# Causal grouped attention: dividing by the row sums on VectorE with 32-block transposes, in place of turning the attended values to tokens and back on TensorE

## What is computed

```python
q = rope(x @ Wq.T + bq); k = rope(x @ Wk.T + bk); v = x @ Wv.T + bv
k = jnp.repeat(k, 4, axis=1); v = jnp.repeat(v, 4, axis=1)
att = jnp.einsum('bhqd,bhkd->bhqk', q, k) / jnp.sqrt(16)
att = jnp.where(causal, att, -jnp.inf)
att = jax.nn.softmax(att, axis=-1)
y = jnp.einsum('bhqt,bhtd->bhqd', att, v)
return y.transpose(0, 2, 1, 3).reshape(b, t, n) @ Wo.T + bo
```

## Time and profile before

| what | value |
|---|---|
| time, median of 3 runs | 1567.59 us (1562.62 to 1567.86) |
| the profiled execution | 1567.11 us, of which span 1565.3 us |
| granted TensorE clock, mean | 0.985 of 2.4 GHz |
| busy over the span: TensorE, VectorE, ScalarE, GpSimd | 92%, 62%, 48%, 36% |
| the stage with the change | about 1075 to 1226 us of the span |
| row maxima start in units 0 to 6 (first L2017) | 1099.58, 1112.49, 1126.84, 1144.32, 1158.66, 1176.15, 1190.47 us |

### The profile page before, as it was taken

How to read it: one execution, slowest core, us unless ns; L and a number is a source line. 1 busy time by engine, 2 the same in 40 slices (tenths; PEclk the granted TensorE clock), 3 DMA queues, 4 the chain that set the end, 5 groups by cost and what they waited for, 6 DMA issues and landing times. The chain is left out here.

```text
span 1565.3 us, 29243 instructions
## 1 busy us (share of the span) xinstructions
PE 1439.8 (92%) x10620; PEld 1117.4 (71%) x10646; DVE 965.8 (62%) x2214; ACT 756.6 (48%) x1877; POOL 561.7 (36%) x556
## 2 busy tenths in 40 slices
PE   6999999999899899899999999998898898988897
PEld 4778777787689767677777766895565596733586
DVE  5666667666575665656565557548655754565663
ACT  5565656656235334343443443452545362598352
POOL 2835629354136254515333101552000173100173
PEclk9999999999999999999999999999999999998998
DMA  4122231222272343303021007335000534121534
GB/s 147 55 90 68 84 101 46 86 63 90 82 313 85 122 130 112 120 6 114 24 74 69 1 1 287 142 120 192 1 1 2 197 102 147 31 60 33 187 99 138
DMA packets 57453, 149.48 MB, mean 95 GB/s; under 512 B 10224, under 2 KB 24688, under 8 KB 57200
## 3 DMA queue, kind: packets, MB, share of 16 engines
q1 hardware_dynamic: 39664, 89.58, 16.7%
q0 software_dynamic: 17664, 58.21, 11.0%
HBM read 104.77 MB, written 38.27 MB: 91 GB/s over the span
## 5 line engine op out<-in xcount | busy, mean ns | idle before, releaser
L145 POOL TENSOR_SCALAR ln_var<-ln_moments 128x4 f32<-128x4 f32 x16 | 4.1, 253 | 403.7 <-DVE ln_moments L130 251.3
L412 POOL DMA_INDIRECT expert_rows<-s_y,s_to_row x92 | 90.9, 989 | 57.9 <-ACT s_y L736 36.9
L1370 ACT ACTIVATE s_scratch<-s_bank,s_neg_max 128x128 f32<-128x128 f32 (+3 forms) x128 | 67.2, 527 | 88.0 <-DVE s_neg_max L1460 87.9
L1460 DVE TENSOR_REDUCE s_neg_max<-s_bank 128x1 f32<-128x128 f32 (+3 forms) x128 | 59.4, 486 | 55.2 <-PE s_bank L1260 55.0
L2797 POOL TENSOR_TENSOR s_w_hi<-s_w_raw,zero 128x1024 fp32r<-128x1024 f32 x25 | 55.6, 2223 | 100.1 <-PE s_memory L81 77.1
L1258 PE MATMUL s_bank<-s_k,s_q 128*128 128x128 f32 (+3 forms) x256 | 88.6, 442 | 1.5 <-DVE s_v L1455 0.8
L2464 ACT ACTIVATE s_exps<-s_bank,s_rms 128x512 f32<-128x512 f32 x128 | 77.9, 690 | 13.5 <-PE s_bank L2363 11.0
L953 DVE TENSOR_TENSOR s_h_e<-s_bank,s_silu_e 128x176 f32<-128x176 f32 x92 | 31.4, 341 | 83.5 <-ACT s_silu_e L724 79.6
L79 PE MATMUL s_bank<-xn_t_hi,s_w_hi 128*128 128x512 f32 x192 | 79.6, 415 | 1.7 <-DVE xn_t_lo L212 1.2
L405 POOL DMA_INDIRECT s_xg<-normed_rows,s_from_row x64 | 63.6, 994 | 38.5 <-DVE s_from_row L848 20.2
L1277 PE MATMUL s_bank<-s_probs_t,s_v 128*128 128x512 f32 (+3 forms) x256 | 74.7, 435 | 2.5 <-ACT s_probs_t L1378 2.5
(11 more groups left out here) (428 smaller groups left out, 4856.4 us busy)
## 6 DMA issues: line engine op xcount, KB each, us to landing
s_expert_w_lo<-experts_lo SPq DMA_DIRECT2D x32, 608.0 KB, 12.9
s_e_lo<-in_experts POOLq DMA_DIRECT2D x32, 304.0 KB, 3.1
experts_hi<-s_e_hi POOLq DMA_DIRECT2D x32, 304.0 KB, 2.5
experts_lo<-s_e_lo POOLq DMA_DIRECT2D x32, 304.0 KB, 2.9
s_expert_w_hi<-experts_hi SPq DMA_DIRECT2D x16, 608.0 KB, 12.1
s_w_raw<-in_wa_o SPq DMA_DIRECT2D x16, 512.0 KB, 3.5
s_yg<-expert_rows SPq DMA_DIRECT2D x32, 256.0 KB, 4.5
s_raw<-in_shared SPq DMA_DIRECT2D x16, 384.0 KB, 6.4
```

Source lines behind the costliest of these rows:

```text
L412: pool.indirect_dma_start(out=y_rows[:, :], out_offset=bass.IndirectOffsetOnAxis(ap=to_row[:, i:i + 1].bitcast(U32), axis=0), in_=y[:, i % ...
L1370: act.activation(probs[:, h % 2, r, 0:(r + 1) * P], score_bank(h, r), ACT.Exp, bias=neg_max[:, 4 * h + r:4 * h + r + 1], accum_out=row_sum ...
L1460: dve.tensor_reduce(neg_max[:, 4 * h + r:4 * h + r + 1], score_bank(h, r), AX.X, ALU.max, negate=True).then_inc(max_done, 1)
```

## The change

The eight transposes per unit on TensorE go, with their two pairs in the ring. VectorE takes the attended values as they lie (head and value on partitions) and does four instructions: a transpose in blocks of 32x32, which puts each query's sum in a column; a reciprocal of these 16 columns; a second transpose by blocks, which reads each reciprocal 32 times and so spreads it over the slot's 32 partitions; and the product. ScalarE's `high_o` and VectorE's `low_o` then read the product in SBUF, where before they read the PSUM bank that was turned back. The last unit's division reads PSUM itself, without `copy_o`. At the end TensorE's fillers become one run of 20 ahead of the last output projection, in place of 5 and 6.

```diff
@@ ring_order
                     if x == 1:
-                        order += [("turn", U - 1)] * (U > 0) + [("q", U + 2)] * (U + 2 < UNITS)
-                    if x == 3:
-                        order += [("back", U - 1)] * (U > 0)
+                        order += [("q", U + 2)] * (U + 2 < UNITS)
...
-            return order + [("turn", UNITS - 1), ("back", UNITS - 1), ("out", len(OUTS) - 1)]
+            return order + [("out", len(OUTS) - 1)]
@@ TensorE
-            def turn_o(U):
...
-            def turn_o_back(U):
...
-                    if j == 0:
-                        if U:
-                            turn_o(U - 1)
-                        if U + 2 < UNITS:
-                            project_q(U + 2)
-                    if j == 1 and U:
-                        turn_o_back(U - 1)
+                    if j == 0 and U + 2 < UNITS:
+                        project_q(U + 2)
...
-            turn_o(UNITS - 1)
-            turn_o_back(UNITS - 1)
-            keep_busy(pe, res, held("back", UNITS - 1)[:, 1, :], 6)
+            keep_busy(pe, res, held("att", UNITS - 1)[:, 1, :], 20)
             project_out(len(OUTS) - 1)
-            keep_busy(pe, res, held("back", UNITS - 1)[:, 1, :], 9)
+            keep_busy(pe, res, held("att", UNITS - 1)[:, 1, :], 9)
@@ ScalarE
             def copy_o(U):
                 act.wait_ge(attended, TB * (U + 1))
                 if U:
-                    act.wait_ge(o_natural, U)
+                    act.wait_ge(o_scaled, U)
...
             def high_o(U):
-                act.wait_ge(o_ready, U + 1)
+                act.wait_ge(o_scaled, U + 1)
...
-                act.activation(o_hi[:, U % 3, :], single("back", U), ACT.Copy).then_inc(o_hi_done, 1)
+                act.activation(o_hi[:, U % 3, :], o[:], ACT.Copy).then_inc(o_hi_done, 1)
...
-            copy_o(UNITS - 1)
             high_o(UNITS - 1)
@@ VectorE
             def scale_o(U):
-                by_head = single("turn", U).rearrange("p (t g s) -> p t g s", t=TB, s=SLOT)
-                dve.wait_ge(o_natural, U + 1)
-                dve.reciprocal(inverse[:], by_head[:, :, :, HD]).then_inc(inverse_done, 1)
+                if U + 1 < UNITS:
+                    dve.wait_ge(o_copied, U + 1)
+                    attended_values = o_raw[:]
+                else:
+                    dve.wait_ge(attended, TB * UNITS)
+                    attended_values = single("att", U)
+                if U:
+                    dve.wait_ge(sums_inverted, U)
+                dve.transpose(by_query[:], attended_values).then_inc(sums_turned, 1)
+                dve.wait_ge(sums_turned, U + 1)
+                if U:
+                    dve.wait_ge(inverse_done, U)
+                dve.reciprocal(by_query_inverse[:], by_query[:].rearrange("p (b r) -> p b r", r=SLOT)[:, :, HD]).then_inc(sums_inverted, 1)
+                dve.wait_ge(sums_inverted, U + 1)
+                if U:
+                    dve.wait_ge(o_scaled, U)
+                dve.transpose(inverse[:], by_query_inverse[:].unsqueeze(2).broadcast_to([P, S // SLOT, SLOT])).then_inc(inverse_done, 1)
                 dve.wait_ge(inverse_done, U + 1)
                 if U:
-                    dve.wait_ge(o_ready, U)
-                dve.tensor_tensor(o[:].rearrange("p (t g s) -> p (t g) s", t=TB, s=SLOT),
-                                  single("turn", U).rearrange("p (t g s) -> p (t g) s", t=TB, s=SLOT),
-                                  spread(inverse[:].rearrange("p t g -> p (t g)"), SLOT), ALU.mult).then_inc(o_scaled, 1)
+                    dve.wait_ge(o_lo_done, U)
+                dve.tensor_tensor(o[:], inverse[:], attended_values, ALU.mult).then_inc(o_scaled, 1)
 
             def low_o(U):
                 dve.wait_ge(o_hi_done, U + 1)
-                dve.tensor_tensor(o_lo[:, U % 3, :], single("back", U), f32(o_hi[:, U % 3, :]), ALU.subtract).then_inc(o_lo_done, 1)
+                dve.tensor_tensor(o_lo[:, U % 3, :], o[:], f32(o_hi[:, U % 3, :]), ALU.subtract).then_inc(o_lo_done, 1)
```

More of the change, by code:

```diff
@@ L1560, in causal_gqa_stage @@
         exps = [sb(f"exps{j}", [P, KV_HEADS, S - j * P]) for j in range(TB)]
-        o_raw, inverse, o = sb("o_raw", [P, S]), sb("inverse", [P, TB, KV_HEADS]), sb("o", [P, S])
+        o_raw, inverse, o = sb("o_raw", [P, S]), sb("inverse", [P, S]), sb("o", [P, S])
+        by_query, by_query_inverse = sb("by_query", [P, S]), sb("by_query_inverse", [P, S // SLOT])
         o_hi, o_lo = sb("o_hi", [P, 3, S], F32R), sb("o_lo", [P, 3, S], F32R)
@@ L1576, in causal_gqa_stage @@
         scores_ready, exp_done = sem("scores_ready"), sem("exp_done")
-        attended, o_copied, o_natural, inverse_done, o_scaled, o_ready, o_hi_done, o_lo_done = (
-            sem("attended"), sem("o_copied"), sem("o_natural"), sem("inverse_done"), sem("o_scaled"),
-            sem("o_ready"), sem("o_hi_done"), sem("o_lo_done"))
+        attended, o_copied, sums_turned, sums_inverted, inverse_done, o_scaled, o_hi_done, o_lo_done = (
+            sem("attended"), sem("o_copied"), sem("sums_turned"), sem("sums_inverted"), sem("inverse_done"),
+            sem("o_scaled"), sem("o_hi_done"), sem("o_lo_done"))
         out_ready, out_added = sem("out_ready"), sem("out_added")
@@ L1652, in read @@
                 return exp_done, scores_count(*at)
-            if kind in ("q", "shift", "att", "turn", "back"):
-                return {"q": q_rotated, "shift": q_shift_done, "att": o_copied, "turn": o_scaled, "back": o_lo_done}[kind], at[0] + 1
+            if kind in ("q", "shift", "att"):
+                return {"q": q_rotated, "shift": q_shift_done, "att": o_copied}[kind], at[0] + 1
             return out_added, at[0] + 1
```

## The result

The changed kernel takes 1588.01 us (median of 4 runs, 1583.61 to 1596.12), the kernel before 1567.72 beside it: +20.3 us, a ratio of 1.014 with a 95% interval of 1.0109 to 1.0172. The forecast was 1573.4, at most 1581. The change makes the kernel slower, by over three times what was walked.

The account below looks back on a forecast made before the run. VectorE was taken to bound each unit up to `attend`, TensorE after it. Units 1 to 5 4.95, unit 6 0.44, unit 7 0.77, the end -0.4: +5.8 us on 1567.59, so 1573.4, range 1566 to 1581.

Parts of the forecast that it names:

- What bounds the kernel: Each unit goes at VectorE's pace from its first row maximum to `attend`, at TensorE's after it.
- The cost on VectorE: Division in each unit: 1.79 us to the product, 0.28 before; `rotate_q` 1.24 us late, `attend` 0.97 in unit 4.
- the open start: When `rotate_q` starts after the product's start: taken as 0.61 us, with 0.75 kept for the range.
- What goes on TensorE: Eight transposes per unit go: `rotate_q`'s 0.19 us wait goes, transposes back worth nothing, shorter ring frees no VectorE time.
- the pause: VectorE's 0.31 us idle ahead of the second row maximum of j = 2; used up, giving back 0.1 us and more.
- Unit 7 and the end: Last division's path +0.77 us; after the last `attend`, a gain of 0.4 us, limited by 20 fillers on TensorE.
- The sum: Whole kernel: 4.95 + 0.44 + 0.77 - 0.4 = +5.8 us, or +0.37%.
- the forecast 0.44 for unit 6: Unit 6, which has no `rotate_q`: `attend` at 1199.79 against 1199.35, 0.44 us late.
- The clock: Rival, chance 0.27: TensorE's clock falls in its waits, up to 1.5 us each; three falls 1578, six 1582.
- the walk at full clock: The forecast's step-by-step timing through the units without falls of the clock: 1573.4 us, own range 1570.5 to 1576.5, chance 0.55.
- TensorE the bound all through: Rival, chance 0.08: TensorE paces whole units, so the removed transposes count, -6.0 us, 1561.6.
- the cost is hidden: Rival, chance 0.10: VectorE's 3.55 us idle per unit takes up the division, 1567.6 us.

Follow-up runs that it names:

- e2: The kernel before, TensorE's transposes kept, with two unread 128x512 block transposes added on VectorE ahead of the product: 1591.41 us, ratio 1.0131.
- e4: The change, with the division moved on VectorE behind a unit's last row maxima, splits and output projections 0 to 2 one unit later: 1555.57 us, ratio 0.992.
- e6: The change without VectorE's two block transposes, reciprocals taken of a tile of ones, so nothing is divided by its sums: 1563.43 us, ratio 0.9988.
- e5: The change plus matmuls of zeros on TensorE: eight ahead of step 3, nine inside step 5, twelve ahead of output projection 3: 1570.54 us, ratio 1.0035.
- run 25: Not a label but a count: the kernel before, unchanged, was run 25 times beside e5 to e7: 1558.99 to 1574.36 us.
- e7: The kernel before, turns kept on TensorE, in the late order: division on VectorE behind a unit's last row maxima, turn back one unit later: 1562.7 us, ratio 0.9967.
- e3: The change, with eight unread transposes a unit put back on TensorE in units 1 to 5, four of them ahead of step 3: 1579.78 us, ratio 1.0076.

## Why the prediction was wrong

*What bounds the kernel:* right. The stage runs at VectorE's pace up to `attend`, and e2, e4 and e6 move just that.

*The cost on VectorE:* right. 1.77 us to the product against 1.79, the open start at 0.61 as taken. The Trainium skill's table (VectorE: DVE Perf Modes, section on the TRN2 errata) gives an estimate of 0.59 us for a transpose; the trace has 0.70 and 0.71, near the 0.72 and 0.71 of stage 7.

*What goes on TensorE:* right in sign, wrong in size. I gave it 0.19 us a unit for `rotate_q` and about 0.1 for the pause; e6 shows 0.6. The ring frees step 5 of its wait for `low_o`, of which I had written that it "frees no VectorE time". Read the other way, the transposes on VectorE cost 15.18 - 13.73 = 1.45 us a unit and what goes on TensorE gives back 0.61: 0.83 net, where 0.97 was forecast.

*Unit 7 and the end:* e5, at full clock, has 8.34 and 8.85 us, +0.72 and -0.38 against 7.62 and 9.23 before (forecast +0.77 and -0.4). In the change itself one fall lay over both: 9.60 and 10.25. The fillers of the end did what they were walked to do, and the last output projection came 0.14 us after its `low_o` (1244.54 + 0.69 = 1245.23, against 1245.37), whose end they cover:

```profile
1241.45 4.26 PE L87 MATMUL s_pair<-zeros 128*128 128x512 bf16 x19 [0.16 <-issue]
...
1244.54 0.69 DVE L2032 TENSOR_TENSOR s_o_lo<-s_o,s_o_hi 128x512 fp32r<-128x512 f32 x1 [0.70 <-ACT s_o_hi L1909]
1245.37 0.47 PE L79 MATMUL s_pair<-s_w_hi,s_o_hi 128*128 128x256 f32 x1
```

*The sum* of +5.8 us without a fall is a little too high. Five times the 0.83 of unit 1, with the 0.72 and -0.38 of e5 and the forecast 0.44 for unit 6, which no run shows at full clock, make 4.9; e5's stage, less its own fillers and its one fall, gives 5.0, and its medians and ratio +3.8 to +5.5.

*The clock,* the step that failed. The prediction held the walk at full clock to be the likeliest (0.55, falls 0.27), on "the stretch is short, and each unit's other half is dense", and its sum has no term for falls. The runs show one in every unit from 2 on, worth 13.2 of the stage's 18.2 us. The trace had the hint: the fall at the stage's start before came behind waits of 1.00 us (at 1091.58) and 1.16 us around sparse work, and the walk itself put a wait of 1.7 us and one of 1.1 into each of five units (measured 1.64 to 1.71, and 0.85 in unit 1). Two more things were off. First the price: up to 1.5 us for a fall, taken from eight fillers, where a unit shows 2.0 (2.80 to 2.91 less 0.83). A fall in the change takes 6.8 us (0.62 and 0.53 in two windows of 4), not only as long as eight fillers. Second the reason: I wrote that the transposes had filled just these places. By e2 they were not enough, and by e6 they were not needed; what differs between the kernels that hold the clock without fillers and those that don't is how long VectorE's chain keeps step 3 waiting (0.16 us in e6; 1.00 and 1.66 in units 3 and 1 of e2, 1.65 to 1.71 in the change). Why unit 1 of the change escapes, and unit 1 of e6 does not, stays open.

*TensorE the bound all through* and *the cost is hidden:* both fall, the first by unit 1, which is 0.83 us longer at full clock with eight transposes fewer. The second became true once the order on VectorE was changed (e4).

What stays open: the time outside the stage. In the profiled execution of the change the first row maximum of unit 0 comes at 1105.97 us, 6.4 later than before, behind stages that the change does not touch; in the nine profiled executions of the experiments it comes between 1095.3 and 1100.3. Part of it is the clock: the stretch below is at 1.2 GHz until 1083 us (0.63 from 1080 to 1084), and its like in the kernel before is half as long (0.59 from 1070 to 1074, then 1.00).

```profile
1076.00:1080.00 4.00, 3.24 (x14) 2.35 (x13) 3.29 (x14) 1.50 (x4) 2.50 (x4) 0.51 0.90 308
```

Such falls differ from one execution to the next, and with them the time: the kernel before, run 25 times beside e5 to e7, scatters over 15 us (1558.99 to 1574.36) at mean clocks of 0.979 to 0.989. The profiled execution of the change (1591.27 us) is itself 3.3 us over its median. So 18.2 us in the stage and 20.3 in the medians of four runs each don't contradict one another.

## What to carry to other kernels

Before work is moved to an engine "with room", look at where in the loop its room is: here 3.5 us of VectorE lay idle per unit, and the four instructions stood elsewhere. Then ask what the waiting engine does meanwhile: a delay of 0.8 us a unit cost TensorE 2 us more by its clock, and matmuls of zeros in the wait brought most of it back. A change that looks bad may be a good one in the wrong place; the same instructions a few lines further down in VectorE's order made the kernel 12 to 14 us faster than before, 7 to 9 of it by the transposes themselves.

## What the runs showed of the hardware

- TensorE fell to 1.2 GHz after waits that are much shorter than the stretch at the low clock: behind waits of 1.65 to 1.71 us (change, units 2 to 5) it stayed there for 6.8 us, behind waits of 0.77 us that follow four transposes (e3) for 3.4 to 6.8 us. The same waits in unit 1 of the change were followed by no fall.
- With transposes on TensorE in or beside the waits the clock fell in all of units 1 to 5 (e2, e3); with matmuls of zeros in both waits of each unit it fell in none of them (e5). These zeros also filled more of the wait than the transposes.
- A block transpose of 128x512 float32 on VectorE takes 0.68 to 0.72 us in the change, from SBUF or PSUM, and also with a source read 32 times over; the dependent instruction starts 0.03 to 0.04 us behind it.
